# An expert kernel's routing table: one half finished two batches later, and the chain for each expert's last tile on GpSimd

## The reference

```python
x = L0_attn_x                                  # (16, 512, 128)
xn = _layernorm(x)
# attention, 16 heads of 8: q and k normalised to length 1, causal
sim = einsum('bhid,bhjd->bhij', q, k) * 8.0
o = softmax(where(causal, -max, sim)) @ v      # then @ Wo
# experts: 8 of them, 512 hidden; each token goes to its best two
probs = softmax(einsum('bsh,eh->bse', xn, Wr))
top_v, top_i = top_k(probs, 2); top_v /= sum(top_v)
for e in range(8):
    out += (gelu(xn @ W1[e].T + b1[e]) @ W2[e].T + b2[e]) * w_e
return x + attention(xn) + experts(xn)
```

## Time and profile before

| what | before |
|---|---|
| median of 3 runs | 851.84 us (846.14 to 852.64) |
| the profiled execution: its time, its span | 851.78 us, 849.9 us |
| busy PE, DVE, ACT, POOL | 723.3 us (85%), 537.0 us (63%), 483.3 us (57%), 438.1 us (52%) |
| first batch of attention on PE | from 107.2 us |
| batches 1 to 7 | one about every 21.7 us, to 290 us |
| expert tiles | about 295 to 640 us |
| mean granted TensorE clock | 0.915 of full speed |

### The profile page before, as it was taken

How to read it: one execution, slowest core, us unless ns; L and a number is a source line. 1 busy time by engine, 2 the same in 40 slices (tenths; PEclk the granted TensorE clock), 3 DMA queues, 4 the chain that set the end, 5 groups by cost and what they waited for, 6 DMA issues and landing times. The chain is left out here.

```text
span 849.9 us, 18967 instructions
## 1 busy us (share of the span) xinstructions
PE 723.3 (85%) x5959; PEld 448.7 (53%) x5959; DVE 537.0 (63%) x1350; ACT 483.3 (57%) x801; POOL 438.1 (52%) x558
## 2 busy tenths in 40 slices
PE   3777578999999789788799959788879999999986
PEld 2555322333333378677699948676768333333322
DVE  7799887888888723333344414443445589999964
ACT  2555468888988633333344413332324798889883
POOL 4444438777777753354400060345530677778772
PEclk9888869999999989798999978987979899999997
DMA  6666655444444444332322222222321334444441
GB/s 195 215 213 195 153 146 123 95 99 97 100 99 96 105 148 135 99 103 86 107 63 68 68 74 62 74 74 73 84 70 51 81 82 104 101 103 107 110 106 32
DMA packets 170227, 89.18 MB, mean 105 GB/s; under 512 B 77216, under 2 KB 159936, under 8 KB 170176
## 3 DMA queue, kind: packets, MB, share of 16 engines
q1 hardware_dynamic: 161984, 71.74, 33.2%
q0 software_dynamic: 8192, 16.79, 7.1%
HBM read 39.47 MB, written 32.24 MB: 84 GB/s over the span
## 5 line engine op out<-in xcount | busy, mean ns | idle before, releaser
L674 ACT ACTIVATE prob<-psum 128x1024 f32<-128x1024 f32 x320 | 312.4, 1027 | 63.3 <-PE psum L766 53.3
L684 ACT ACTIVATE prob<-psum,prob 128x256 f32<-128x256 f32 x284 | 116.3, 473 | 245.9 <-PE psum L905 181.3
L791 PE MATMUL psum<-prob,v 128*18 128x384 f32 (+2 forms) x2560 | 181.7, 393 | 4.4 <-DVE prob L1178 1.8
L917 PE MATMUL psum<-prob 128*128 128x128 f32 x1136 | 155.4, 291 | 33.0 <-ACT prob L684 19.9
L550 POOL DMA_INDIRECT rows<-slot_y,idx x128 | 123.9, 968 | 101.8 <-DVE acc L1231 65.7
L917 PEld LDWEIGHTS psum<-prob 128*128 128x128 f32 x1136 | 150.4, 206 | 45.0 <-issue 18.6
L905 PE MATMUL psum<-xs,prob 128*128 128x256 f32 x568 | 152.8, 417 | 20.6 <-DVE xs L1308 17.3
L552 POOL DMA_INDIRECT slot_x<-rows,idx x128 | 128.0, 1000 | 79.7 <-DMA rows<-xn_rows 42.2
L766 PE MATMUL psum<-qks 32*128 32x512 f16 (+3 forms) x1024 | 126.7, 308 | 16.2 <-ACT prob L674 9.9
L563 POOL TENSOR_SCALAR_AFFINE_SELECT prob<-prob 128x512 f32<-128x512 f32 x128 | 90.4, 706 | 96.1 <-ACT prob L674 95.6
L905 PEld LDWEIGHTS psum<-xs,prob 128*128 128x128 f32 x568 | 112.9, 209 | 39.6 <-issue 14.3
(11 more groups left out here) (141 smaller groups left out, 701.1 us busy)
## 6 DMA issues: line engine op xcount, KB each, us to landing
xs<-slot_x SPq DMA_DIRECT2D x71, 128.0 KB
slot_y<-xs SPq DMA_DIRECT2D x71, 128.0 KB
xs<-in_L_attn_x SPq DMA_DIRECT2D x16, 256.0 KB, 3.5
prob<-in_L_ffn_W SPq DMA_DIRECT2D x16, 256.0 KB, 3.2
xn_rows<-xns SPq DMA_DIRECT2D x16, 256.0 KB, 3.4
xn_cols<-xts SPq DMA_DIRECT2D x16, 256.0 KB, 3.6
xt<-xn_cols SPq DMA_DIRECT2D x16, 256.0 KB
rows<-xn_rows SPq DMA_DIRECT2D x16, 256.0 KB, 2.9
```

Source lines behind the costliest of these rows:

```text
L674: act.activation(prob[:, q % 2, KEPT[u], :], score[(q + u) % 2], ACT.Exp, scale=SCALE / UP ** 2).then_inc(exp_done, 1)
L684: act.activation(hs[:, s, c, :], psum[:, 2 * s + c // 2, (c % 2) * FT:(c % 2 + 1) * FT], ACT.Gelu, bias=ws[:, s, B1C + c:B1C + c + 1]).the ...
L791: mm = pe.matmul(ps_octet[w // 2][32 * g:32 * g + VW, first:first + cols], lhs, prob[:, w % 2, KEPT[u], c:c + cols], start=(i == 0 and not ...
L917: mm = pe.matmul(psum[:, 6 + s, j * D:(j + 1) * D], hs[:, s, c, j * P:(j + 1) * P], ws[:, s, W2C + c * D:W2C + (c + 1) * D], start=(c == 0 ...
```

## The change

The chain for `last_i` leaves DVE and runs on POOL as 15 instructions, since two fused ones are split. It starts when DVE raises a new semaphore, `ends_ready`. On DVE the ranking is cut by halves. DVE ranks and places the first half, picks its slots and raises `routed`; then it only ranks the second half (which reads the ranks out of PSUM), clears `ps_o`, and raises a new semaphore, `ranked`, for which PE now waits in place of `routed`. The rest of the second half is done in batch 2: `place_half(1)` in step 0, one choice of `slots_half(1, ...)` in steps 1 and 2, and then `routed` is raised again. SP and POOL wait for this second one at the start of `between`. The scratch `place` and `mine` moves to the buffer `xs`, which attention's first half doesn't use otherwise. PE's, ACT's and SP's instructions are otherwise the same.

```diff
-        mine = rows[:, 0, 1].rearrange("p t (u e) -> p (t u) e", e=E)
-        place = rows[:, 1, 1].rearrange("p t (u e) -> p (t u) e", e=E)
+        place = xs[:, 1, 0].rearrange("p t (u e) -> p (t u) e", e=E)
+        mine = xs[:, 1, 1].rearrange("p t (u e) -> p (t u) e", e=E)
...
-        lasts_ready, routed = sems("lasts_ready routed")
+        ends_ready, last_step, lasts_ready = sems("ends_ready last_step lasts_ready")
+        ranked, routed = sems("ranked routed")
...
             def between():
+                sp.wait_ge(routed, 2)
...
+            steps = 0
+
+            def stepped(ins):
+                nonlocal steps
+                steps += 1
+                ins.then_inc(last_step, 1)
+                pool.wait_ge(last_step, steps)
+            pool.wait_ge(ends_ready, 1)
+            sizes = cnt[:, 1, :, E:]
+            pool.tensor_scalar(lastf[:, 1], counts[:, 1], 0.0, None, ALU.is_gt)
+            pool.tensor_scalar(mark[:, 0, :], sizes[:, 1], 0.0, None, ALU.is_gt)
+            pool.tensor_scalar(mark[:, 1, :], sizes[:, 2], 0.0, None, ALU.is_gt)
+            stepped(pool.tensor_tensor(lastf[:, 0], ends[:, 1], ends[:, 0], ALU.subtract))
+            stepped(pool.tensor_tensor(lastf[:, 0], lastf[:, 0], mark[:, 0, :], ALU.mult))
...
+            stepped(pool.tensor_scalar(lastf[:, 0], lastf[:, 0], 1.0 / FT, -1.0, ALU.mult, ALU.add))
+            stepped(pool.tensor_tensor(lastf[:, 2], lastf[:, 0], back[:], ALU.add))
+            stepped(pool.tensor_scalar(lastf[:, 3], lastf[:, 2], -float(FFN_TILES + E), None, ALU.add))
+            stepped(pool.tensor_tensor(lastf[:, 3], lastf[:, 3], lastf[:, 1], ALU.mult))
+            stepped(pool.tensor_tensor(lastf[:, 3], lastf[:, 3], back[:], ALU.subtract))
+            pool.tensor_scalar(last_i[:], lastf[:, 3], float(FFN_TILES + E), None, ALU.add).then_inc(lasts_ready, 1)
...
             def between():
+                pool.wait_ge(routed, 2)
...
                             if known(b, 0):
-                                pe.wait_ge(routed, 1)
+                                pe.wait_ge(ranked, 1)
...
-            dve.tensor_tensor(begins[:], ends[:], sizes, ALU.subtract)
-
-            dve.tensor_scalar(lastf[:, 1], counts[:, 1], 0.0, None, ALU.is_gt)
-            dve.tensor_scalar(mark[:, 0, :], sizes[:, 1], 0.0, None, ALU.is_gt)
-            dve.tensor_scalar(mark[:, 1, :], sizes[:, 2], 0.0, None, ALU.is_gt)
-            stepped(dve.tensor_tensor(lastf[:, 0], ends[:, 1], ends[:, 0], ALU.subtract))
...
-            stepped(dve.scalar_tensor_tensor(out=lastf[:, 3], in0=lastf[:, 2], scalar=-float(FFN_TILES + E),
-                                             in1=lastf[:, 1], op0=ALU.add, op1=ALU.mult))
-            dve.scalar_tensor_tensor(out=last_i[:], in0=lastf[:, 3], scalar=float(FFN_TILES + E), in1=back[:],
-                                     op0=ALU.add, op1=ALU.subtract).then_inc(lasts_ready, 1)
+            stepped(dve.tensor_tensor(begins[:], ends[:], sizes, ALU.subtract))
+            dve.sem_inc(ends_ready, 1)
+            stepped(dve.tensor_tensor(begins[:], begins[:], upto[:, 0:3], ALU.subtract))
+            stepped(dve.tensor_tensor(jumps[:], begins[:, 1:3], begins[:, 0:2], ALU.subtract))
             dve.wait_ge(placed, 1)
             dve.wait_ge(norms_ready, NB)
-            for h in range(2):
-                some_tiles = slice(h * T // 2, (h + 1) * T // 2)
-                ranks = ps_pc.rearrange("p (t e) -> p t e", e=E)[:, some_tiles, :]
-
-                def of_half(ap):
-                    return ap[:, h:h + 1, :].broadcast_to([P, T // 2, E])
-                dve.tensor_tensor(logits[:, some_tiles, :], ranks, of_half(upto[:, 1:3]), ALU.is_ge)
-                stepped(dve.tensor_tensor(place[:, some_tiles, :], ranks, of_half(begins), ALU.add))
-                stepped(dve.tensor_tensor(logits[:, some_tiles, :], logits[:, some_tiles, :], of_half(jumps), ALU.mult))
-                stepped(dve.tensor_tensor(place[:, some_tiles, :], place[:, some_tiles, :], logits[:, some_tiles, :],
-                                          ALU.add))
+            halves_of = [slice(h * T // 2, (h + 1) * T // 2) for h in range(2)]
+
+            def of_half(ap, h):
+                return ap[:, h:h + 1, :].broadcast_to([P, T // 2, E])

+            def rank_half(h):
+                ranks = ps_pc.rearrange("p (t e) -> p t e", e=E)[:, halves_of[h], :]
+                dve.tensor_tensor(logits[:, halves_of[h], :], ranks, of_half(upto[:, 1:3], h), ALU.is_ge)
+                stepped(dve.tensor_tensor(place[:, halves_of[h], :], ranks, of_half(begins, h), ALU.add))
+
+            def place_half(h):
+                past_jump, to = logits[:, halves_of[h], :], place[:, halves_of[h], :]
+                stepped(dve.tensor_tensor(past_jump, past_jump, of_half(jumps, h), ALU.mult))
+                stepped(dve.tensor_tensor(to, to, past_jump, ALU.add))

+            def slots_half(h, c):
+                some_tiles = halves_of[h]
+                stepped(dve.tensor_tensor(mine[:, some_tiles, :], hot[:, c, some_tiles, :], place[:, some_tiles, :],
+                                          ALU.mult))
+                with nc.allow_low_precision(reason="one number that isn't zero, and whole"):
+                    stepped(dve.tensor_reduce(slots[:, some_tiles, c], mine[:, some_tiles, :], AX.X, ALU.add))
+
+            rank_half(0)
+            place_half(0)
             for c in range(TOPK):
-                dve.tensor_tensor(mine, hot[:, c], place, ALU.mult).then_inc(r_step, 1)
-                dve.wait_ge(r_step, next_step())
-                with nc.allow_low_precision(reason="one number that isn't zero, and whole"):
-                    dve.tensor_reduce(slots[:, :, c], mine, AX.X, ALU.add).then_inc(r_step, 1)
-                dve.wait_ge(r_step, next_step())
-
-            dve.memset(ps_o, 0.0).then_inc(r_step, 1)
-            dve.wait_ge(r_step, next_step())
+                slots_half(0, c)
             dve.sem_inc(routed, 1)
+            rank_half(1)
+            stepped(dve.memset(ps_o, 0.0))
+            dve.sem_inc(ranked, 1)
...
                     if known(b, 1) and w == 1:
                         write_plan()
+                    if known(b, 2) and w == 0:
+                        place_half(1)
+                    if known(b, 2) and w in (1, 2):
+                        slots_half(1, w - 1)
+                        if w == 2:
+                            dve.sem_inc(routed, 1)
```

13 lines of the change are left out of this document (4 added, 9 removed).

## The result

| | before | after |
|---|---|---|
| median, 11 runs each, one beside the other | 852.53 us (846.14 to 856.91) | 856.18 us (852.09 to 860.84) |
| ratio, 95% interval | | 1.0066 (1.0038 to 1.0093) |
| profiled execution: time, span | 851.78 us, 849.9 us | 855.25 us, 853.3 us |
| `begins` starts on DVE | 106.43 | 104.30 |
| PE starts batch 1 | 136.27 | 136.07 |

The change makes the kernel slower, by about 0.7%: 3.65 us between the medians, 5.6 by the ratio.

The account below looks back on a forecast made before the run. Attention was taken as limited by TensorE, its start by DVE's routing chain, for which PE waits twice. Sum: 851.78 − 0.7 + 1.0 = 852.1, stated as 852.0 us; range 847.0 to 856.0.

Parts of the forecast that it names:

- DVE's side: Routing on DVE at the start of attention: `ranked` at 112.5 instead of 117.1, with 3.1 us of room.
- The gain offered: PE's two waits on DVE's routing chain, 1.52 us before the first `weigh` and 0.85 before a projection: 2.37 us.
- the gain goes through: Rival, chance 0.20: SP's queue drains faster and 2.37 us is kept, 850.4 us; with a higher clock, 848.1.
- POOL's chain: Fifteen small instructions for `last_i` on POOL: 3.9 us taken, 7.2 at most; `last_i` 1.8 us later.
- my low case: POOL's chain at 0.20 us per instruction plus 11 steps of 0.08: 3.9 us.
- POOL takes about twice DVE's time: Rival, chance 0.15: 0.30 us per POOL instruction, chain 4.5 us, `last_i` 2.4 late, 0.2 kept: 852.6 us.
- the POOL chain is slow: Rival, chance 0.15: 0.48 us per instruction, `last_i` 5.1 late, 2.6 lost at batch 1 and 1.0 in batch 2: 855.4 us.
- SP's queue: Paddings, `acc` load and batch 1's transposes wait behind `last_i` on SP: batch 1's operands ready at 135.5, limiting PE.
- the slack of 2.1 us: Before batch 1: operands ready at about 134.2 in the old trace, PE begins at 136.27.
- gives nearly the same limit: POOL waits for all paddings before its first scatter, so it can start at most 0.8 us earlier.
- Batches 2 and 3: `place_half(1)` in batch 2 delays PE's projection: 1.0 us taken, at most 1.8; `slots_half` costed at nothing.
- my −0.7 for the start of batch 1: Of the 2.37 us offered, 0.7 is kept, since PE starts batch 1 at 135.5 instead of 136.27.

Follow-up runs that it names:

- e3: Changed kernel with the second half's pieces moved ahead of DVE's copy of v in the first preparation of batches 1, 2 and 7: 853.53 us, ratio 1.0025.
- e4: Changed kernel with SP's load of the first half of `acc` moved behind batch 1's transposes: 853.71 us, ratio 1.0000.
- e10: The changed kernel, unchanged, run again on another chip: 769.56 us beside 765.17, ratio 1.0051.
- e15: Kernel of e5 with the chain for the last tiles on POOL again: 763.62 us, ratio 0.9966.
- e14: Kernel of e5 with the second half's pieces back in batch 2 behind the copy of v: 762.94 us, ratio 0.9960.
- e9: The kernel before, unchanged, run again on another chip: ratio 0.9998.
- e1: Changed kernel with the chain for the last tiles back on DVE: 855.54 us beside 852.37, ratio 1.0048.
- e8: Changed kernel with the edits of e1 and e3, SP's order as in the changed kernel: 765.62 us, ratio 1.0002.
- e11: Kernel of e8 with 18 products of batch 0's scores computed once more in the wait for batch 1's transposes: 767.14 us, ratio 1.0018.
- e7: Changed kernel with 18 matmuls that nobody reads added at the end of batch 0: 775.14 us, ratio 1.0120.
- e5: Changed kernel with the edits of e1, e3 and e4 together: 761.06 us beside 765.14, ratio 0.9941.
- e6: Kernel before with only SP's load of `acc` moved behind batch 1's transposes: 764.64 us, ratio 0.9987.
- e12: Kernel of e5, run once more on another chip: 761.50 us, ratio 0.9944.
- e2: Kernel before with only the chain for `last_i` moved to POOL, routing not halved: 854.35 us, ratio 1.0025.

## Why the prediction was wrong

I forecast 852.0 us with a range up to 856.0, so next to no change; 856.18 was measured, and the interval of the ratio excludes no change. The direction of the loss stood only in my rivals. Step by step:

- **DVE's side was right.** The scale of batch 1 follows the increment of `ranked` at 110.37, on the scale of before 112.50; I said 112.5. PE's first `weigh` and the projection lost their idle. The multiplies beside POOL's small chain took 0.43 us, so DVE wasn't held up.
- **The gain offered was larger than I said.** With PE no longer idle at 117 the clock rose there (1.00 in 117.10:121.80), and the projection comes at 118.54 + 2.13 = 120.67 instead of 123.91: 3.2 us early and not 2.37. I had that mechanism only in the rival in which the gain goes through.
- **POOL's chain: the contention was on its side.** I took 3.9 us, it took 109.17 − 104.63 = 4.54, and `last_i` came 2.4 late instead of 1.8. I had asked only what POOL does to DVE. These rows of POOL and DVE in after show the reverse:

```profile
105.83 0.20 POOL L542 TENSOR_TENSOR lastf<-lastf,ends 128x8 f32<-128x8 f32 x1
106.48 0.38 POOL L544 TENSOR_TENSOR lastf<-lastf,mark 128x8 f32<-128x8 f32 x1
107.41 0.20 POOL L546 TENSOR_SCALAR lastf<-lastf 128x8 f32<-128x8 f32 x1
...
106.38 0.42 DVE L1168 TENSOR_TENSOR xs<-xs,logits 128x256 f32<-128x256 f32 x1
106.84 0.42 DVE L1172 TENSOR_TENSOR xs<-hot,xs 128x256 f32<-128x256 f32 x1
107.30 0.42 DVE L1175 TENSOR_REDUCE slots<-xs 128x32 int32<-128x256 f32 x1
```

L544 starts while DVE's L1168 runs, an operation with two inputs in SBUF, and ends 0.06 us after it; beside the reduction L1175, with one input, L546 takes 0.20. Four POOL instructions start under such a two-input operation (L543, L544, L545, L548). They take 0.29 to 0.38, 1.35 us together where four times 0.20 would be 0.80. The same four take 0.30, 0.38, 0.38 and 0.30 in `e3`, `e4`, `e10` and `e15`. Without that 0.55 the chain is 3.99 us, the 3.9 of my low case. In batch 2 it is DVE that waits: the two operations of `place_half` took 0.73 and 0.74 beside a scatter and a select on POOL, and once (`e14`, at 160.33) one took 1.81, beside two selects. By the rule of the Trainium skill ("SBUF — State Buffer", Who interferes with whom) both places should have suffered; the trace agrees for both, in the first on POOL and in the second on DVE.
- **The chain time of the rival "POOL takes about twice DVE's time" was met by luck.** 4.54 against DVE's 2.30 is 1.97 times, and 1.96 is the figure in the Trainium skill ("GPSIMD Engine Reference", Elementwise — side-by-side cycle accounting), for one large add. Here it is reached only with the 0.55 us above, and with 15 instructions against 13. In the rival "the POOL chain is slow" I also put the limit at 0.33 us per instruction; by my own sum a `last_i` 2.5 late is 15 × 0.31.
- **SP's queue: the step that failed.** I let the delay shift batch 1's operands to 135.5. They came at 136.07 + 2.13 = 138.2. Of the 2.7 us between, 0.6 is POOL's chain, held up by DVE as above. About 0.9 is the issue of the transposes, which I carried over unchanged: 10.44 instead of 9.90 for the first three, and 0.87 and 1.52 instead of 0.57 and 1.25 for the two behind. And 1.2 is the way from the end of issue to use: 3.1 us, where I took batch 0's 1.9. In the runs it lies between 2.5 (`e10`) and 4.7 (`e9`). I took a duration from batch 0, where in the trace of before the DMA engines moved 200 GB/s (98.5 to 107.2), and used it where POOL's scatters and the load run as well and they moved 273 (120.4 to 132.0). With 3.1, the slack of 2.1 us that I saw in the trace of before would have been 0.9, and the early gain was gone.
- **POOL "gives nearly the same limit": seen, and costed at nothing.** I said that POOL can start at most 0.8 us earlier; it was 0.9. But PE came 3 us earlier to the mask, so the rest of it, 2.05 us, became an idle in one piece.
- **Batches 2 and 3: four times what I took.** Forecast +1.0 to +1.8. From the mark of batch 2 to that of batch 4 after takes 47.9 us and before 43.7: 4.2 more, 3.3 of them up to the mark of batch 3. The rows give it: 0.96 for transposes, 1.65 more at the projection (1.93 for 0.28), and 1.5 us that three rows took longer at 1.2 GHz (1.30, 0.61 and 1.91 at 173.89 to 177.5, for 0.84, 0.39 and 1.06). Only the second is the mechanism I named; the wait for batch 2's transposes and the clock I hadn't.
- **The term that was missing.** I reckoned idle as idle. Before, once the clock had risen (1.00 from 122.5 on), PE's idles in batch 0 were 0.85, 1.15 (at 132.14) and 1.33 us, and the clock held. The change gathered them into 2.05 and 4.12. Behind them PE did 3.93 us of work at 1.2 GHz, 2 us lost. The sum for the mark of batch 2 then is 1.9 (138.2 − 136.27) + 2.0 = 3.9; measured 3.6. So my −0.7 for the start of batch 1 became +1.9, the clock behind it added 2.0, and my +1.0 for batch 2 became 4.2: 8.1 against the 7.8 measured from `begins`, of which the earlier start gave back 2.1.

The rival "the POOL chain is slow", 855.4 us, is nearest to the time, but for a reason that wasn't there: with its steps an instruction took 0.30 us, not 0.48. The 7.8 us lost from `begins` to batch 4 became 5.7 at the first gelu through the earlier start, and 3.4 at the end of the profiled execution: the second half of attention took 189.5 us against 192.5, at a granted clock of 0.97 against 0.95. No run isolates that last part, and the ratio of the times (5.6 us) suggests that it belongs to these two executions.

What stays open: the early start of 2.1 us (last section); why the clock held in `e14` behind the two waits behind which it fell in `e4` and `e10`; and why the issue-to-use time of the transposes varies between 2.5 and 4.7 us in kernels whose queues look alike.

## What to carry to other kernels

Before freeing an engine that another waits for, follow each later release of the waiting one (here a mask, a queue and a copy) and ask whether it moves too; if not, the gain returns as one long idle, and PE's clock goes with it. A slack read from one trace must be wider than the scatter of the duration it is built on, above all for DMA. Mend the fixed releases first, or with it: the early DVE work was worth nothing without the order on SP, that order nearly nothing without the early work, and both with the pieces in covered places gave 4.3 us.

## What the runs showed of the hardware that I hadn't expected

- **The clock falls behind short idles too, and not always.** Wherever it was full in the first half of attention, it went to 0.50 behind (or, in `e1`, `e8` and `e11`, at the end of) every single idle of 1.85 to 4.42 us. Single idles up to 1.33 us didn't take it. Behind the pair of 1.16 and 1.35 us it fell in `e4` and `e10` and held in `e14`, with the same instructions around it. It came back 3.4 (`e1`, at 176) to 9.7 us (`e4`, at 177) after the idle's end, under attention's own work, but not during the 7.9 us of the first filler (`e7`).
- **A load's length in a queue shows behind it.** The issue of the 2 MB `acc` load took 0.92 us, but the first transpose behind it took 7.22 to issue. In the runs where the load was moved away (`e4`, `e5`, `e6`, `e12`, `e14`, `e15`), every transpose of batch 1 took 1.23 to 1.51.
- **Small POOL arithmetic costs nearly the same for all kinds**, 0.20 to 0.27 us on 128x8 with 0.08 between dependent steps, unless it starts under a DVE operation with two inputs in SBUF: then it ended 0.05 to 0.11 us after that one (0.29 to 0.38 in after, up to 0.65 in `e2`).
- **The first stage doesn't take the same time in all kernels**, though its instructions are the same. `begins` starts at 104.30 and 103.93 in the changed kernel and at 104.20 and 104.38 in `e3` and `e4`; at 106.43 and 106.06 in the kernel before and at 106.3 to 106.6 in `e1` and `e2`; in the others between 104.8 and 106.6. Where one kernel was run twice (before, the changed one, `e5` and `e12`), its two starts lie within 0.4 us. In the window 80 to 90 the granted clock is 0.90 to 1.00 in the first four and 0.83 in the kernel before, `e1` and `e2`. The cause wasn't tried.
- **Chips differ by 87 us in one kernel**: 852 on the first, 765 on the two others. Of that, 82 lie in the expert tiles: 358 us against 276 from the first gelu to the second half of attention. On the slower chip PE idles more there (window 310 to 600: busy 245.75 us in 290 at clock 0.90, on the faster 281.25 at 0.98). The cause wasn't tried. All comparisons above are within one chip or by ratios.
